# A two-layer convolution-like block on one core: the next batch's load and first normalisation made earlier, and norms, searches and layer norms put at other steps

## The reference, cut to what matters

```python
def _L0_conv_ref(x, negative_dict):          # 256 words of 256 channels
    f_norm = x / jnp.linalg.norm(x, axis=1, keepdims=True)
    d_norm = negative_dict / jnp.linalg.norm(negative_dict, axis=1, keepdims=True)
    sim = jnp.einsum('bchw,nc->bnhw', f_norm, d_norm)
    dist = (1.0 - sim) * 0.5
    apm = jnp.min(dist, axis=1, keepdims=True)
    index = jnp.argmin(dist, axis=1)
    replace_map = (apm < THRESHOLD).astype(x.dtype)          # 0.625
    restructured = jnp.transpose(negative_dict[index], (0, 3, 1, 2))
    return x * (1.0 - replace_map) + restructured * replace_map

def _L1_conv_ref(x, ...):
    xn = layer_norm(xf, norm_g, norm_b)      # over the 256 channels of each pixel
    chunks = ...                             # 4 chunks of 64 channels, each a sequence of 1024
    ym = mamba(chunks, ...) + skip_scale * chunks
    y = layer_norm(y, norm_g, norm_b)
    return einsum('blc,oc->blo', y, proj_w) + proj_b

def mamba(...):                              # 128 inner channels, 16 states each
    xc = silu(conv4(xi) + conv_b);  dt = softplus(...);  A = -exp(A_log)
    h = exp(dt_t * A) * h + (dt_t * x_t) * B_t               # for t in 1024 steps
    y = (h @ C_t + xc * D_param) * silu(z);  out = y @ out_proj_w.T

x = x + _L0_conv_ref(_gn(x), ...)
x = x + _L1_conv_ref(_gn(x), ...)
```

## Time and profile before

| | |
|---|---|
| median of three runs | 4,431.4 us |
| profiled execution: time, span | 4,433.55 us, 4,431.7 us |
| busy: PE, DVE | 3,779.5 us (85%), 4,003.7 us (90%) |
| busy: ACT, POOL | 2,810.5 us (63%), 3,427.9 us (77%) |
| granted TensorE clock, mean | 0.932 |
| DMA, 16 engines | 65.7% busy, mean 170 GB/s |

### The profile page before, as it was taken

The page is one execution under the profiler, slowest core; times in us unless marked ns, Lnnn a source line. Parts: engine busy times, 40 slices in busy tenths (PEclk is TensorE's granted clock), DMA queues, the critical chain, the costliest instruction groups (busy, mean ns, idle before and its releaser), DMA issues. The chain is left out here.

```text
span 4431.7 us, 44302 instructions
## 1 busy us (share of the span) xinstructions
PE 3779.5 (85%) x13840; PEld 1269.6 (29%) x13840; DVE 4003.7 (90%) x3073; ACT 2810.5 (63%) x3528; POOL 3427.9 (77%) x2086
## 2 busy tenths in 40 slices
...
GB/s 39 154 143 193 149 189 177 174 192 152 190 157 188 201 135 202 148 192 180 167 197 143 200 159 186 201 140 202 140 196 183 164 197 144 198 162 186 193 166 109
DMA packets 217723, 751.74 MB, mean 170 GB/s; under 512 B 27400, under 2 KB 28816, under 8 KB 213392
## 3 DMA queue, kind: packets, MB, share of 16 engines
q1 hardware_dynamic: 217488, 748.91, 65.7%
...
## 5 line engine op out<-in xcount | busy, mean ns | idle before, releaser
L592 POOL TENSOR_TENSOR state<-state,c_all 128x1024 f32<-128x1024 f32 x1024 | 2400.1, 2362 | 252.0 <-DVE state L953 229.5
L953 DVE TENSOR_TENSOR_SCAN state<-dtb,ub 128x1024 f32<-128x1024 f32 x1024 | 2341.0, 2286 | 42.7 <-ACT dtb L795 6.1
L1182 PE MATMUL ub<-u,spr 64*128 64x512 f32 x4096 | 1271.5, 683 | 352.1 <-DVE state L953 349.6
L795 ACT ACTIVATE dtb<-dtb,a_neg 128x1024 f32<-128x1024 f32 x1024 | 1159.7, 1141 | 389.4 <-DMA dtb<-dt_scratch 379.8
L944 DVE TENSOR_TENSOR ub<-ub,b_all 128x1024 f32<-128x1024 f32 x1024 | 1243.1, 1214 | 105.0 <-PE ub L1182 98.8
L1182 PEld LDWEIGHTS ub<-u,spr 64*128 64x128 f32 x4096 | 347.8, 196 | 1160.2 <-DVE state L953 679.6
L1198 PE MATMUL yp<-state,gat 128*32 128x512 f32 x4096 | 583.0, 643 | 6.1 <-POOL state L592 6.1
L1047 PE MATMUL mb<-xs,wtap 128*128 128x512 f32 x512 | 261.4, 657 | 20.1 <-DMA xs<-xn 10.6
L668 ACT ACTIVATE dt<-mb 128x512 f32<-128x512 f32 x128 | 75.8, 592 | 241.7 <-PE mb L1078 241.7
L643 ACT ACTIVATE e_x<-mb,ncb 128x512 f32<-128x512 f32 x128 | 88.0, 687 | 219.1 <-PE mb L1047 219.1
L1061 PE MATMUL mb<-xc,wdt 128*128 128x512 f32 x256 | 153.1, 683 | 78.3 <-ACT ym L715 55.4
(11 more groups left out here) (143 smaller groups left out, 4821.6 us busy)
## 6 DMA issues: line engine op xcount, KB each, us to landing
dtb<-dt_scratch SPq DMA_DIRECT2D x1024, 512.0 KB, 4.8
xs<-xn SPq DMA_DIRECT2D x128, 256.0 KB, 5.3
b_all<-bc_scratch SPq DMA_DIRECT2D x64, 512.0 KB, 6.4
c_all<-bc_scratch SPq DMA_DIRECT2D x64, 512.0 KB, 7.9
xt<-in_x SPq DMA_DIRECT2D x16, 1024.0 KB, 6.6
x_scratch<-xt SPq DMA_DIRECT2D x16, 1024.0 KB, 7.0
...
dt_scratch<-dt SPq DMA_DIRECT2D x128, 128.0 KB, 3.6
```

The source lines that it names most:

```text
L592: pool.tensor_tensor(v, v, c_all[:, c % 2, :], ALU.mult).then_inc(gated, 1)
L795: act.activation(dtb[:, k, :], dtb[:, k, :], ACT.Exp, scale=a_neg[:, GROUP[g]:GROUP[g] + 1]).then_inc(decayed, 1)
L953: dve.tensor_tensor_scan(state[:, g % STATES, :], dtb[:, k, :], ub[:, g % 2, :], 0.0, ALU.mult, ALU.add).then_inc(scanned, 1)
L1182: last = pe.matmul(ub[:, g % 2, h * HALF:(h + 1) * HALF], spr[lo:lo + TURN, GROUP[g] % 8, :], u[lo:lo + TURN, c % 2, h * HALF:(h + 1) * HA ...
```

## The change

The work is the same; its places differ.

- The first group norm of a batch and its load (the ten names in `EARLY`) move from sequence 0, one batch ahead, to sequences 2 and 3, two batches ahead: `x_in` at (2, 24), sums at (3, 1) and (3, 3), affines at (3, 22) and (3, 23). Batch 1's are done in the prologue, on each engine behind the prologue's last `prep_` work and ahead of the first decay, spread, multiply and gate. The last but one batch (`PENULT`) leaves them out.
- The norm halves move from (0, 26), (0, 28) to (0, 0), (0, 2). The sims, nears, picks and hots are taken apart: one by one in sequence 0 instead of all at its end.
- The layer-norm statistics of both kinds move: `c_mean`, `c_square` to (0, 30), (0, 31), (1, 1), (1, 2), `a_mean`, `a_square` to (2, 3), (2, 4), (2, 8), (2, 9). `post_take` is at j = 14 in every sequence, and `post_out` of sequence 1 at 12.
- `Banks` counts every batch by itself; the order in which banks are opened is the only thing that it gives back.
- Two waits on `s_x2ld` on ScalarE go; others cover them.

```diff
-PE_BATCH = {(0, 11): ["a_group0"], (0, 12): ["post_out"], (0, 26): ["a_norm0"], (0, 28): ["a_norm1"],
...
+PE_BATCH = {(0, 0): ["a_norm0"], (0, 2): ["a_norm1"], (0, 9): ["a_sim00", "a_sim01"], (0, 10): ["a_sim10", "a_sim11"],
...
-SP_BATCH = {(0, 4): ["x_in"], (0, 15): ["xs3"], (0, 17): ["x2_back"], (2, 2): ["x2_store"], (2, 6): ["out"],
-            (2, 13): ["xs0"], (2, 17): ["xs1"], (2, 20): ["out_wait"], (3, 15): ["xs2"]}
+SP_BATCH = {(0, 15): ["xs3"], (0, 20): ["x2_back"], (1, 24): ["x2_store"], (2, 2): ["out"], (2, 15): ["out_wait"],
+            (2, 20): ["xs0"], (2, 21): ["xs1"], (2, 24): ["x_in"], (3, 15): ["xs2"]}
+EARLY = ("x_in", "a_sum00", "a_sum01", "a_group0", "a_gm0", "a_mom0", "a_rstd0", "a_newton0", "a_affine00",
+         "a_affine01")
...
+        if kind == PENULT and name in EARLY:
+            continue
...
-                t = b + 1
+                t = b + 2 if c == NC - 1 and name in EARLY else b + 1
...
-                        at_least(act, s_x2ld, 16 * b)
...
+            for name in ("a_sum00", "a_sum01", "a_rstd0", "a_affine00", "a_affine01"):
+                do(name, "pre", -1, NC - 1)
             decay(0, 0, 0)
```

More of the change, by code:

```diff
@@ L450, in do @@
                 elif name == "x_in":
-                    await_(a_sqd[1], NJ * t)
-                    await_(s_x2st, 16 * t)
-                    sp.dma_start(xt[:], x_v[t]).then_inc(s_x, 16)
+                    await_(a_sqd[1], NJ * (b + 2))
+                    await_(s_x2st, 16 * (b + 2))
+                    sp.dma_start(xt[:], x_v[b + 2]).then_inc(s_x, 16)
                 elif name == "x2_store":
@@ L476, in _ @@
                 load_chunk(c, 0, "pro", -1)
+            do("x_in", "pre", -1)
             store_bc(0, 0)
@@ L481, in _ @@
                 load_unit(0, 0, g)
-            turn(FIRST, 0)
-            for b in range(1, NB - 1):
-                turn(LOOP, b)
-            turn(LAST, NB - 1)
+            for b in range(NB):
+                turn(kind_of(b), b)
             do("x2_back", "tail", NB)
@@ L609, in _ @@
                 do(name, "pro", -1, NC - 1)
-            turn(FIRST, 0)
-            for b in range(1, NB - 1):
-                turn(LOOP, b)
-            turn(LAST, NB - 1)
+            for name in ("a_mom0", "a_newton0"):
+                do(name, "pre", -1, NC - 1)
+            for b in range(NB):
+                turn(kind_of(b), b)
             do("c_scale0", "tail", NB, 0)
@@ L1016, in _ @@
                 do(name, "pro", -1, NC - 1)
-            turn(FIRST, 0)
-            for b in range(1, NB - 1):
-                turn(LOOP, b)
-            turn(LAST, NB - 1)
+            do("a_gm0", "pre", -1, NC - 1)
+            for b in range(NB):
+                turn(kind_of(b), b)
             for name in ("post_gate", "c_var0", "c_ctr0", "c_var1", "c_ctr1", "c_out00", "c_out01", "c_out10", "c_out11"):
@@ L1168, in do, with sequence_ready @@
                     last.then_inc(m_full[bank], 1)
-            def sequence_ready(kind, b, c):
+            def sequence_ready(turn_of, c):
                 for q in range(2):
-                    bank, use = banks(kind, b, (f"prep_dt{q}", c))
+                    bank, use = banks(turn_of, turn_of, (f"prep_dt{q}", c))
                     pe.wait_ge(m_free[bank], use)
```

61 lines of the change are left out of this document (25 added, 36 removed), and 33 rows, old and new, of tables (ACT_BATCH, DVE_BATCH, PE_BATCH).

## The result

The changed kernel takes 4,549.4 us (median of 4 runs, 4,538.9 to 4,558.6), the kernel before 4,432.3: a ratio of 1.026 with a 95% interval of 1.024 to 1.029. I had forecast 4,374 with a range up to 4,455. The sign is wrong, and the time lies beyond the slower rival too (4,461).

A forecast was written before the change was run, and what follows sets the result against it. VectorE bounds: 252 us of work in a 267 us batch, only 15 us of waits winnable. Waits of 10.7 save 4.3 in 14 batches (60), batch 0 saves 5, prologue and last batch add 6: 4,374 us, range 4,305 to 4,455.

The forecast's parts named there:

- the slower rival: Half clock in front of xc: norms and c_mean1 leave TensorE at 1.2 GHz; 4,461 us, chance 0.17.
- The places that it named: Steps, written sequence.step, counted from 0, where VectorE was to wait; the waits of all terms summed to 10.7 us per batch.
- the signs of being wrong: Listed trace marks: `ub` over 150 or under 60 us, slow norm1, xc over 5 us, dtb line over 20 us.
- the transfers' line: Sign of the transfers rival (4,402 us, chance 0.10): a wait line "state <- dtb" of more than 20 us.
- Prologue: Before the first decay: batch 1's sums to affines on ScalarE make that decay 5.3 us later.
- steps 0.0 to 0.3: Start of sequence 0, norm halves, sum and xc between spreads on TensorE: bounds 0 and 3.9 us per batch, taken 2.2.
- c_mean1: Step 1.0: it waits for c_ctr0's bank with the next spread queued behind; bounds 0 and 2.2 us, taken 0.8.
- the statistics of sequence 2: Step 2.2: square0 makes var0 late and xc waits for a_ctr0's bank; bounds 1.9 and 3.6 us, taken 2.2.
- The second rival: Same as the slower rival: half clock at norms, c_mean1, words and xc; 16.7 us per batch, 4,461 us, chance 0.17.
- turn, keep and words: Steps 1.4 to 1.6: TensorE waits about 2 us for a_oht1; bounds 0 and 2.2 us per batch, taken 0.7.
- x_in with prep_u1: Sequence 3: x_in ahead of step 3.0's dtb row, prep_u1 behind the affines; bounds 0 and 2 us, taken 0.4.
- Third search: Step 0.14: its a_near2 stands behind z's sigmoid and a decay; bounds 0 and 1.1 us per batch, taken 1.1.

The follow-up runs named there:

- e6: Changed kernel with each norm product 64 columns wide instead of 1, same places: 4,487.5 us, ratio 1.012 to the kernel before.
- e2: Changed kernel with c_mean1 moved from the second place of step 1.0 to the first of step 1.1, behind a spread: 4,499.3 us, ratio 1.015.
- e12: Changed kernel with only x_in's issue moved, from half-step 24 to half-step 5 of sequence 2: 4,517.3 us, ratio 1.018.
- e15: Changed kernel with x_in at half-step 5 of sequence 2 and a_xn0, xs0, xs1 at 16, 17, 18: 4,493.4 us, ratio 1.014.
- e14: Changed kernel with sequence 1's second-group sums, group product, a_gm1 and prep_dt1 placed as in the kernel before: 4,529.1 us, ratio 1.022.

## Why the prediction was wrong

**Places: right as far as the list went.** The places that it named (0.3, 0.4, 0.15, 1.2, 1.7, 1.8, 2.4) are in the trace, and `best` fell to the number given. 2.15, 1.12 and 1.13 were not on it. Of the signs of being wrong, three came true: `ub` over 150 us, norm1 at 3.57 in most batches, and xc over 5 us in 2.2; so did the transfers' line of more than 20 us, under the name "issue".

**Prologue: smaller than forecast.** ScalarE's chain took 13.3 us, as I had it, but began at 144.72 us and not at 147.65, so the first scan is at 159.2, 2.2 us later than before and not 5.3. Batch 0, put at 5 us less, takes 260.6 us against 261.3.

**Sizes at half clock: wrong, the largest error.** In the sum, steps 0.0 to 0.3 had 2.2 of bounds 0 to 3.9, c_mean1 0.8 of 0 to 2.2, the statistics of sequence 2 2.2 of 1.9 to 3.6. Measured: 4.35, 2.24 and 3.44. The first came out over its upper end, the second at it, the third just under it. The step that failed is "it is not the rule either: 2.2, a little over the middle". I took the share of slow norm halves in before (7 of 15 second halves) as a chance that carries over. With other neighbours it was 13 of 15, with spread, sum and spread at half clock too. e6 shows the size: wider products, same places, 62 us less. The row that said so was the earlier trace rows, and I had read it right and then priced it at half.

The second rival had these three as one case, at a chance of 0.17, with "the four upper ends seldom meet in one batch" against it: in the means over 14 batches all three are there. The fourth, turn, keep and words, is not: under 0.2 of its 2.2. Right sizes here would not have given the right sign by themselves: 10.7 + 4.8 is 15.5 against 15.0, which by the prediction's own sum is about 4,440 us, near before's time. The rest of the loss is in the terms below.

The Trainium skill, "TensorE: Matmul & The Clock Gate", section "A second HAM failure mode: psum-queue depth-cycling", had the direction: matmul groups that pause for banks make the clock go back and forth. The trace of after agrees at 1.1 and 2.2 (3.75 and 5.37 us behind 4.28 and 2.07 us of idle), and that of e2 only in part, as xc is at full clock behind the same 2.07 us in 11 of 15 batches. For the norms the trace adds that the fall can come with no pause to speak of: in batch 5 only 0.29 us of idle stands between the two halves.

**Transfers: wrong by 3.4 us a batch, with the affines 4.2.** "0, with up to 1 if not" for xs0 and xs1, and "bounds 0 and 2, taken 0.4" for x_in with prep_u1. Measured 3.75 in 2.15 and 3.0, and 0.80 in 3.13, where before has next to nothing. The step that failed: I priced x_in by the difference of two landing times, each measured with little beside it, and xs0 and xs1 by VectorE having had no wait for a decay where they went. I left out that the row for 3.0 must wait for the stores of dt, which land 3.7 us later beside the moved loads. What the change does is to put 1 MB of x_in, 1 MB of xs (four loads of 256 KB), the stores of dt and the loads for b and c within four steps of one another. e12 and e15 split it: 32 us and 24.

**ScalarE in sequence 1: missed.** I wrote of the moments only for sequence 3. They stood at nothing in the sum, with no reason given. a_sum10 and a_sum11 moved by three and two half-steps in the diff, past two decays, and prep_dt1 moved too; neither is in my list. Measured: 1.87 us a batch in 1.12 and 1.13, and 20 us of the kernel (e14).

**Small terms.** Third search 1.39 for 1.1; turn, keep and words under 0.2 for 0.7, and 1.7 and 1.8 2.17 for 1.1: together 0.9 over.

In sum: 10.7 forecast, 23.7 measured; of the 13.0 between them, 4.8 are the three places of the clock, 4.2 the transfers with the affines of 3.13, 1.9 the moments, and 2.1 many small ones. Two terms were too high: turn, keep and words by 0.5, c_out by 0.3.
